# A gated cross-attention layer with routed experts on one core: the second batch's column sum added once by VectorE, first row sums moved, last product in two halves

## The reference

```python
x = x + tanh(g_xattn) * matmul(fake_quant(layernorm(x)), fake_quant(ctx))
x = x + tanh(g_ffn) * ffn(layernorm(x))
...
def fake_quant(x, scale, zp):
    q = clip(round(x / scale + zp), 0, 255)
    return (q - zp) * scale
...
# ffn: shared expert (512 wide) + the chosen two of 16 experts (256 wide) per token
z = silu(xt @ sw1 + sb1) * (xt @ sw2 + sb2) @ sw3 + sb3
h = silu(xt @ w1 + b1) * (xt @ w2 + b2);  y = y + gate[:, None] * (h @ w3 + b3)
```

## Time and profile before

| | before |
|---|---|
| median of 3 runs | 316.20 us (315.91 to 316.38) |
| profiled execution | 316.27 us |
| its span, first to last instruction | 314.3 us |
| mean granted TensorE clock | 0.998 |
| TensorE matmul busy | 293.9 us (94%) |
| VectorE busy | 222.8 us (71%) |
| ScalarE busy | 114.9 us (37%) |
| GpSimd busy | 24.3 us (8%) |
| SP's queue, share of 16 DMA engines | 36.0% |

### The profile page before, as it was taken

One profiled execution on the slowest core, in us unless ns is written; L12 is line 12 of the kernel. 1 busy time (PEld: TensorE's weight loads), 2 busy tenths in 40 slices (PEclk: granted clock), 3 DMA queues, 4 the chain that ended last, 5 costly groups with the idle time before them and its releaser, 6 DMA issues.

```text
span 314.3 us, 4647 instructions
## 1 busy us (share of the span) xinstructions
PE 293.9 (94%) x1868; PEld 149.4 (48%) x1868; DVE 222.8 (71%) x392; ACT 114.9 (37%) x130; POOL 24.3 (8%) x34
## 2 busy tenths in 40 slices
PE   0388999999999999999999999999999999999993
PEld 0224598954544445544444444444444444444441
DVE  2898987895898953685475988868784769659110
ACT  2998558769653540210343305302015040100000
POOL 2010200000002210000000011100101110000000
PEclk9999999999999999999999999999999999999999
DMA  7999970248710753000897600000000000600302
GB/s 277 413 325 346 301 219 6 82 136 168 230 60 0 136 106 95 2 2 0 250 306 250 229 39 2 0 0 0 2 0 0 2 1 0 255 15 1 133 33 104
DMA packets 35700, 35.56 MB, mean 113 GB/s; under 512 B 16068, under 2 KB 30428, under 8 KB 35548
## 3 DMA queue, kind: packets, MB, share of 16 engines
q1 hardware_dynamic: 35664, 35.23, 36.0%
q10 hardware_dynamic: 12, 0.00, 0.0%
HBM read 27.88 MB, written 4.20 MB: 102 GB/s over the span
## 4 chain that ended last, share of the span: by engine, by line
PE 83%; DVE 9%; DMA 3%; ACT 2%; SPq 1%; POOL 1%; issue 1%; DVEq 0%
PE PS L1532 26%; PE PS L1374 20%; PE PS L1565 12%; PE PS L1558 7%; PE PS L1409 7%; PE PS L1321 4%; DMA X<-in_x_dram 3%; PE PS L1390 2%; DVE stats L778 2%; PE PS L1398 2%; PE PS L1328 1%; DVE S2f L814 1%; POOL lnR L474 1%; DVE X L844 1%; DVE wrow L853 1%; DVE area L810 1%
## 5 line engine op out<-in xcount | busy, mean ns | idle before, releaser
L1374 PE MATMUL PS<-areaT,areaW 128*128 128x512 f16 x288 | 62.6, 379 | 0.0
L1374 PEld LDWEIGHTS PS<-areaT,areaW 128*128 128x128 f16 x288 | 28.0, 98 | 33.3
L1532 PE MATMUL PS<-areaT,area 128*128 128x512 f16 x192 | 42.1, 379 | 0.0
L1532 PE MATMUL PS<-areaT,areaW 128*128 128x512 f16 x192 | 42.1, 379 | 0.0
L1321 PE MATMUL PS<-area,areaQ 128*128 128x512 f16 x128 | 32.0, 400 | 1.6 <-DVE area L810 1.5
L1042 DVE SCALAR_TENSOR_TENSOR X<-PS,cf,X 128x512 f32<-128x512 f32 x22 | 15.5, 746 | 20.0 <-PE PS L1565 15.2
L1532 PEld LDWEIGHTS PS<-areaT,area 128*128 128x128 f16 x192 | 18.8, 98 | 22.7
L1532 PEld LDWEIGHTS PS<-areaT,areaW 128*128 128x128 f16 x192 | 18.8, 98 | 22.7
L778 DVE BATCH_NORM_STATS2 stats<-X 128x6 f32<-128x512 f32 x32 | 20.5, 683 | 4.5 <-DMA X<-in_x_dram 4.3
L1558 PE MATMUL PS<-SW,areaH 128*128 128x512 f16 x96 | 21.9, 379 | 0.0
L1321 PEld LDWEIGHTS PS<-area,areaQ 128*128 128x128 f16 x128 | 12.6, 102 | 17.8 <-DVE area L810 3.6
(11 more groups left out here) (187 smaller groups left out, 408.6 us busy)
## 6 DMA issues: line engine op xcount, KB each, us to landing
areaT<-in_ctx_dram SPq DMA_DIRECT2D x12, 512.0 KB, 8.1
ring<-in_L_ffn_sw_dram SPq DMA_DIRECT2D x12, 512.0 KB, 5.5
X<-in_x_dram SPq DMA_DIRECT2D x8, 512.0 KB, 7.6
ring<-in_L_ffn_ew_dram SPq DMA_DIRECT2D x16, 256.0 KB, 5.6
out_dram<-X SPq DMA_DIRECT2D x7, 512.0 KB, 2.7
ring<-in_ctx_dram SPq DMA_DIRECT2D x4, 512.0 KB, 3.8
ring<-in_L_ffn_ew_dram SPq DMA_DIRECT2D x2, 1024.0 KB, 5.0
areaQ<-gate_dram SPq DMA_DIRECT2D x1, 1024.0 KB, 6.8
```

The lines of the kernel that those rows point to most:

```text
L1374: last = mm(PS[:, SU_BANK[half * SC + c] + w, lo:hi], SW[:, wp, 2 * c + w, k, :], XT[:, xp, k, tk], start=(k == 0 and n == 0), stop=(k == ...
L1532: last = mm(PS[:, EU_BANK[u] + w, :], W12S[j][:, wp, k, cs], XT[:, xp, k, b * S:(b + 1) * S], start=(k == 0 and n == 0), stop=(k == KC - 1 ...
```

## The change

Three edits, and the semaphores that they need.

1. Batch 1's column correction. column_sums is no longer called for tiles 4 to 7. Instead column_row multiplies a matrix of ones with S2 once, two matmuls of 512 columns into banks 6 and 7, and add_row on VectorE adds these banks, times the new coefficient cf[:, 14:15], to X for each of the four tiles, before attend. Batch 0 keeps column_sums.
2. Batch 0's bias transpose and row sums move on TensorE from the middle of tile 2's products to transpose_tokens(2), between the high and the low transposes; on VectorE row_terms(0) and shared_biases() move from behind attend(1) to behind ln2_lo(3).
3. The last product is computed in two halves of 256 columns in two banks (last_product), evicted by two operations of 256 columns (last_halves). The output rows of tiles 4 and 5 are stored in two and three pieces: two stores more in all.

```diff
         EVICTIONS = 2 * (len(EVICT[0]) + len(EVICT[1]))
-        STORES = NT + 1
+        STORES = NT + 3
         U = ring[:, :, :].rearrange("p a n -> p (a n)").rearrange("p (u n) -> p u n", n=512)
...
             return (6, 7, 0, 1, 2, 3, 4, 5)[(step_no(b, name, pair) - 1) % 8]
+        LAST_BANK = (6, 7, 0, 1, 2, 3, 4, 5)[STEPS % 8]
...
         sbr_in, sb_T, sbT_rdy = sem("sbr_in"), sem("sb_T"), sem("sbT_rdy")
-        r1_done = sem("r1_done")
+        r1_done, t_done, t_read = sem("r1_done"), sem("t_done"), sem("t_read")
         at_done, at_read = sem("at_done"), sem("at_read")
...
         u0_rdy = sem("u0_rdy")
+        dn_first, y_first = sem("dn_first"), sem("y_first")
         dn_done, y_rdy, y_out, rows_fin = sem("dn_done"), sem("y_rdy"), sem("y_out"), sem("rows_fin")
...
                     sp.wait_ge(at_done, TB)
+                    sp.wait_ge(r1_done, 1)
                 sp.dma_start_transpose(Q1T[:, i % TB, :, :], QB[:, i % 2, :]).then_inc(q1t_in[i % 2], 16)
...
                         store(pair)
-            sp.wait_ge(y_rdy, evict_no(1, "X11f", 1))
-            store(TB + 1, slice(0, 512))
+            for pair in range(2):
+                sp.wait_ge(y_rdy, evict_no(1, "X11f", pair))
+                store(TB + pair, slice(0, 512))
             sp.wait_ge(y_rdy, evict_no(1, "X12f", 0))
-            store(TB)
+            store(TB, slice(512, D))
+            sp.wait_ge(y_first, 1)
+            store(TB + 1, slice(512, 768))
             sp.wait_ge(y_rdy, evict_no(1, "X12f", 1))
-            store(TB + 1, slice(512, D))
+            store(TB + 1, slice(768, D))
...
                 act.wait_ge(su_done, u + 1)
+                if u == 0:
+                    act.wait_ge(sbT_rdy, 2)
                 if u >= 2:
...
                 v.tensor_scalar(sbT[:, 1, :], PS[:, 3, 8 + SC:8 + 2 * SC], UPS, None, ALU.mult).then_inc(sbT_rdy, 1)
+                dve.wait_ge(sbT_rdy, 2)
...
                 dve.wait_ge(at_read, i + 1)
+            def add_row(i):
+                dve.wait_ge(t_done, 1)
+                Xi = X[:, i, :].rearrange("p (h n) -> p h n", h=2)
+                v.scalar_tensor_tensor(Xi, PS[:, 6:8, :], cf[:, 14:15], Xi, ALU.mult, ALU.add).then_inc(t_read, 1)
...
                 v.tensor_tensor(dst, dst, u, ALU.add).then_inc(y_rdy, 1)
+            def last_halves(x):
+                dve.wait_ge(y_rdy, evict_no(1, "X12u", 1))
+                dve.wait_ge(dn_first, 1)
+                v.scalar_tensor_tensor(x[:, 0:256], PS[:, bank_of(1, "P3", 1), 0:256], cf[:, 11:12], x[:, 0:256], ALU.mult,
+                                       ALU.add).then_inc(y_first, 1)
+                dve.wait_ge(dn_done, STEPS)
+                v.scalar_tensor_tensor(x[:, 256:512], PS[:, LAST_BANK, 0:256], cf[:, 11:12], x[:, 256:512], ALU.mult,
+                                       ALU.add).then_inc(y_rdy, 1)
...
                     from_bank(b, "X11f", p, x11[p], "P2", x11[p], "X11u")
-                for p in range(2):
+                for p in range(2 - b):
                     from_bank(b, "X12f", p, x12[p], "P3", x12[p], "X12u")
+                if b:
+                    last_halves(x12[1])
...
             link(v.tensor_scalar(cf[:, 6:7], cf[:, 7:8], cf[:, 8:9], float(D), ALU.mult, ALU.mult))
+            link(v.tensor_scalar(cf[:, 14:15], cf[:, 4:5], cf[:, 8:9], None, ALU.mult))
             coefs(0, 1, None, XS, None)
             attend(1)
-            row_terms(0)
-            shared_biases()
             lo_chunk("sw", 0)
...
             ln2_lo(3)
+            row_terms(0)
+            shared_biases()
             lo_chunk("sw", 4)
...
             su_gate(3)
+            dve.wait_ge(x_int, NT)
+            for i in range(TB, NT):
+                add_row(i)
+            dve.wait_ge(t_read, TB)
             lo_chunk("sw3", 0)
...
                 for h in range(2):
-                    mm(PS[:, AT_BANK[i] + h, :], Q1T[:, i % TB, k, :], Q2[:, k, h * 512:(h + 1) * 512],
-                       start=(k == 0), stop=False)
+                    last = mm(PS[:, AT_BANK[i] + h, :], Q1T[:, i % TB, k, :], Q2[:, k, h * 512:(h + 1) * 512],
+                              start=(k == 0), stop=(i >= TB and k == KC - 1))
+                if i >= TB and k == KC - 1:
+                    last.then_inc(at_done, 1)
+            def column_row():
+                pe.wait_ge(s2_rdy, B)
+                pe.wait_ge(su_hf, 2)
+                for h in range(2):
+                    last = mm(PS[:, 6 + h, :], onesh[:, :], S2[:, h * 512:(h + 1) * 512], start=True, stop=True)
+                last.then_inc(t_done, 1)
...
             def row_sums(b):
-                if b == 0:
-                    pe.wait_ge(q1_rdy, TB)
-                else:
+                if b:
                     for j in range(2):
                         pe.wait_ge(q1t_in[j], 32)
-                    pe.wait_ge(at_read, TB)
+                    pe.wait_ge(r1_rdy, 1)
+                    pe.wait_ge(sbT_rdy, 2)
                 for j in range(TB):
...
                 pe.wait_ge(sbr_in, 32)
+                pe.wait_ge(at_read, TB)
                 nc.tensor.transpose(PS[:, 3, 8:16], sbr[:, :], idf[0:8, 0:8]).then_inc(sb_T, 1)
...
                 last.then_inc(tk_T, 1)
+                if i == 2:
+                    bias_columns()
+                    row_sums(0)
                 pe.wait_ge(ln_lo, i + 1)
...
                 products(2, k)
-                if k == 3:
-                    pe.wait_ge(q1_rdy, TB)
-                    bias_columns()
-                    row_sums(0)
             column_sums(2)
-            pe.wait_ge(r1_rdy, 1)
-            pe.wait_ge(sbT_rdy, 2)
+            pe.wait_ge(q1_rdy, TB)
             for k in range(4):
...
                     shared_up(0, c, w)
+            column_row()
             row_sums(1)
             pe.wait_ge(q2_rdy, 2 * KC)
-            pe.wait_ge(s2_rdy, 2)
             for i in range(TB, NT):
...
                     pe.wait_ge(su_hf, SC)
+                if i == NT - 1:
+                    pe.wait_ge(t_read, TB)
                 for k in range(KC):
                     products(i, k)
-                column_sums(i)
...
+            def last_product():
+                piece, blk = PRODUCT["P3"]
+                free_bank(1, "P3", 1)
+                for half, bank in enumerate((bank_of(1, "P3", 1), LAST_BANK)):
+                    if half:
+                        pe.wait_ge(y_rdy, evict_no(1, READ_LAST["P5"], 0))
+                    o, cs = PS[:, bank, 0:256], slice(half * 256, half * 256 + 256)
+                    for c in range(SC):
+                        for n, (hp, wp) in enumerate(((0, 0), (1, 0), (0, 1))):
+                            mm(o, HT[:, hp, c, P:2 * P], SW3[:, wp, c, 512 + half * 256:768 + half * 256],
+                               start=(c == 0 and n == 0), stop=False)
+                    for c in range(HC):
+                        a = pieces(1, 0, c, PIECE[piece], 1), pieces(1, 1, c, PIECE[piece], 1)
+                        for n, (hp, wp) in enumerate(((0, 0), (1, 0), (0, 1))):
+                            last = mm(o, a[hp][:, 0, 1, :], W3B[BLOCK[blk]][:, wp, c, cs], start=False,
+                                      stop=(c == HC - 1 and n == 2))
+                    last.then_inc(dn_done if half else dn_first, 1)
             pe.wait_ge(h_lo, 8)
...
                 product(1, "P2", pair, (pair, 0))
-            for pair in range(2):
-                product(1, "P3", pair, (pair, 1))
+            product(1, "P3", 0, (0, 1))
+            last_product()
```

## The result

The changed kernel took 319.28 us (median of 6 runs, 317.95 to 319.95), the kernel before 315.85 us in the runs beside it: ratio 1.0107, 95% interval 1.0082 to 1.0133. It is slower by 3.4 us; that is 0.8 us under the forecast of 320.1 and inside the range. The profiled execution took 317.95 us (span 316.1), the shortest of the six; its mean granted clock is 0.994, that of the other five 0.989.

The account below looks back on a forecast made before the run. TensorE was taken to bound the kernel from about 51 us, with VectorE only 2.6 us ahead at sd_evac(0). 316.27 + 2.4 + 1.9 - 0.5 = 320.1 us, own range 318.9 to 321.5; 317.7 to 321.2 including the unchanged-clock case.

Parts of the forecast that it names:

- The first part: Moved batch 0 row sums: TensorE starts its unbroken work at tile 2's low transposes 0.15 us earlier.
- Covered, by some 0.2 us: Stage from 84 us: S2 complete at 85.08, before column_row can start at 85.4, so its 0.1 us delay is hidden.
- VectorE 5.0 us late: From attend(4) on, VectorE runs late: 0.3 us row sums plus 4.9 four passes over X, less 0.2 absorbed.
- The wait: Fourth shared_down tile: TensorE idles 5.5 us for sd_evac(0), starting 2.4 us later (bounds 2.2 to 2.8).
- The clock: Behind TensorE's idle stretch: clock falls, nine matmuls run at twice the pitch, costing 1.9 us (0 to 5.2).
- Rival A: Fourth shared_down tile: the wait is there, but the clock stays up; 318.2 us, chance 0.30.
- The third part: Last product in halves: matmuls 0.05 us more, shorter last eviction and store; together -0.5 us (-0.2 to -0.6).
- half of that is 0.3 us at most saved, 0 at least: Last store: 128 KB instead of 256, which kept the 16 queues busy 0.74 us; saving 0 to 0.3 us.
- The pitch of the halves: Last product: matmuls of 256 columns take 0.109 us each by proportion, 3.93 against 3.88 us in all.
- The sum: Whole kernel: 316.27 us profiled, plus 2.4 wait, plus 1.9 clock, minus 0.5 last product, gives 320.1 us.
- Rival B: VectorE's idle time between 86 and 114 us takes in two of the four passes; faster, 312.6 us, chance 0.06.

Follow-up runs that it names:

- rows_only: Kernel before with only the move of batch 0's row sums and bias transpose: 315.65 us, ratio 0.9987.
- filled_wait: Whole change plus 24 unread matmuls of 512 columns keeping TensorE busy in front of its wait for sd_evac(0): 316.89 us, ratio 1.0029.
- earlier_eviction: Whole change with sd_evac(0) moved two places ahead in VectorE's list, between bn(7) and ln2_lo(6): 314.85 us, ratio 0.9958.
- halves_only: Kernel before with only the last product in halves, evicted and stored separately, and tile 4's store in two pieces: 313.88 us, ratio 0.9943.
- split_store: Kernel before with its last store issued as two of 256 columns, product and eviction unsplit: 315.91 us, ratio 0.9994.
- branch_later: Kernel before with TensorE's instruction stream held ahead of its final branch until VectorE's last eviction: 317.0 us, ratio 1.0057.
- without_column: Whole change with the column-sum part undone, leaving the moved row sums and the last product in halves: 313.63 us, ratio 0.9918.
- early_eviction: Whole change with sd_evac(0) one place further ahead in VectorE's list, before the last low part: 313.43 us, ratio 0.9924.

## Why the prediction came out, and where it didn't

**The first part** (-0.15): borne out by this profile, but not shown. 50.36 against 50.68 is -0.32; 0.17 of it was there already at the first rows of this execution, before the edit acts, and the rest is the 0.15 written. But the unchanged kernel's two profiles lie 0.24 us apart at the same place (50.68 and 50.92), and rows_only can't tell its time from that of the kernel before. "Covered, by some 0.2 us", said of S2, failed: S2 came 0.41 us later and TensorE waited 0.32. It cost nothing at the end, since TensorE waited for VectorE afterwards anyway; on VectorE it is part of the next term.

**VectorE 5.0 us late**: 5.3 at attend(4), 5.28 at sd_evac(0) (120.36 against 115.08). The four passes take 4.85 us in the timeline after, as worked out; the 0.3 over is S2's lateness, through the row sums (row_terms(1) 0.60 us late for the 0.3 written). The mechanism, the one wait that decides, and its end near 121.4 (121.6) were right. **The wait** was 5.47 for 5.5, and the tile is 2.8 us late for 2.4: inside the bounds 2.2 to 2.8, at their end. That the wait's length came out to 0.03 us is luck, since both of its ends lay later than written: TensorE was ready at 116.3 instead of 115.8 (0.32 us of it the wait for S2) and let go at 121.8 instead of 121.4.

**The clock** (+1.9, 0 to 5.2): 1.45 in the profiled execution, with six matmuls of 634 ns where nine were taken from the start of the kernel, and 2.4 in the median by filled_wait. Rival A, the clock that stays up, was wrong in all six runs (mean clock 0.989 to 0.994, against 0.995 to 1.000 in the recorded runs of the kernel before); its time of 318.2 lies near the 317.95 of the profiled execution for another reason, the end. The Trainium skill, "TensorE: Matmul & The Clock Gate", section What's actually happening, says that the number of slow matmuls varies between runs; the six mean clocks, 0.994 once and 0.989 five times, agree with it, and so do earlier_eviction's 1.000 to 0.988.

**The third part** (-0.5, -0.2 to -0.6): this is the term that failed. It measured -2.1 in halves_only and -2.46 at the end of the profiled execution. The sentence "half of that is 0.3 us at most saved, 0 at least" took the store's landing for the time that its bytes need. But the landing was 4.1 us by the trace, with the bytes through in 0.8, and 2 us of it were one DMA engine's packets behind an instruction fetch. In the window of the earlier trace rows this stood already to be read: after it, up to the end of the span, lay another 2.7 us that no sum over bytes explains. The pitch of the halves was right: 1.31 us for 12 matmuls of 256 columns is 0.109.

**Why halving helps**, as far as shown: not by the size of the store (split_store, branch_later). With the halves both fetches of TensorE's branch fall elsewhere: one between the last two stores, the other 1.3 us after the last one's packets. They do so because TensorE's stream comes to its branch later against the last eviction: 3.2 us ahead of it in the kernel before (305.81 against 309.01), 1.2 us ahead in halves_only (307.59 against 308.82) and in the whole change (312.06 against 313.29).

```profile
L1646 PEldq COMPARE_BRANCH  x1: 3999/3999/3999, 307.6 to 307.6; - x1
...
L1656 PEldq COMPARE_BRANCH  x1: 3671/3671/3671, 312.1 to 312.1; - x1
...
L45 SPq COMPARE_BRANCH  x1: 38/38/38, 315.8 to 315.8; - x1
```

Why the stream runs ahead of the matmuls by just so much wasn't tested. The rows show a limit, too: in the whole change the branch ends at 315.7 and SP's wait for the last store at 315.8, and in halves_only the branch ends last (311.6 against 311.4). A still quicker last store would gain next to nothing there.

**The sum**, in the profiled execution's terms, is 316.27 + 2.8 + 1.45 - 2.46 = 318.1 for 317.95 measured, where the forecast had +2.4, +1.9 and -0.5: the end 2.0 and the clock 0.5 too dear, the wait 0.4 too cheap. The median lies 1.3 above that execution, with a lower clock (0.989 against 0.994). In medians the end gave 2.1 (halves_only) for 0.5, while the wait with 2.8 for 2.4 and the clock with 2.4 for 1.9 cost more than written: errors of opposite sign, so the total came out partly by luck.

**Rival B** (faster if VectorE is under 3.1 us late) had the right form: with sd_evac(0) in the idle time before L869 VectorE is 1.9 us late there (116.98 against 115.08), and the change pays, 313.43 us. It is the fastest median of all, 0.2 below without_column, whose interval it overlaps: most of its gain over before is the third part's.

## What to carry to other kernels

When work moves from TensorE to VectorE, look for the one eviction behind that list which frees TensorE's next bank, and move it into a pause of VectorE's; then look what it delays, since one place further ahead gave back about half of the gain over the kernel before (ratio 0.9958 after 0.9924). Price an idle stretch of TensorE with its clock: here 5.5 us idle cost 2.8 us by the wait and about 2.4 by the clock. And read a store's landing beside its packets: what it takes over its bytes' time belongs to something else, which may be moved.

## What the runs showed of the hardware

A 16 KB instruction fetch shares a DMA engine with a store's packets, and these wait for its end: one engine of 16, eight packets of 128, and 1.4 to 2.2 us more until the last store's last packet (seven profiles; with 1 KB and 2 KB packets alike). It happens in mid-kernel too: in filled_wait a 256 KB store and one of the regular fetches began together, the fetch ended 1.34 us later, and eight packets started at 1.33. In early_eviction it is the same: a regular fetch ends at 307.60, and the last eight packets of the 256 KB store beside it start then. That they share an engine is read from these coincidences and from branch_later; the records name no engine.

TensorE's branch over the loop for further experts, at the end of the kernel, took 3.6 to 4.3 us in all 14 profiles, with a 16 KB fetch in it. In branch_later that was the last thing to end, 2.7 us after SP's wait for the last store.

TensorE's clock fell also behind a short pause: in earlier_eviction, with some 3 us of 32-column and 16-column matmuls of the router and a wait of 1.62 us ahead, it was at its lower level from 127.1 us on in the profile, and seven of the ten runs have a mean clock of 0.995 or less. Behind the wait of 1.79 us in early_eviction, which matmuls of 512 columns precede and follow, it stayed up in the profile, and the mean clock is 1.000 in all four runs.
